# A residual addition moved from VectorE to TensorE and ScalarE, in the attention across heads of a fused two-layer kernel

## The reference

```python
x = x + attn_b(layernorm(x))
def attn_b(x):                       # 16 heads of 8 features
    q = x @ Wq + bq
    k, v = split((x @ Wdown + bdown) @ Wup + bup)
    ...  # rope turns all heads of a token alike, so it drops out of q.k and the kernel leaves it out
    att = einsum('bthd,btgd->bthg', q, k) / sqrt(8)   # per token, head against head
    att = softmax(att, axis=-1)
    out = einsum('bthg,btgd->bthd', att, v)
    return out.reshape(B, T, D) @ Wout + bout
```

## Time and profile before

| | |
|---|---|
| Time, median of 3 runs | 1090.13 us (1087.06 to 1095.89) |
| The profiled execution's own time | 1098.24 us |
| Its span | 1096.5 us |
| Mean granted TensorE clock | 0.955 of full speed |
| TensorE (PE) busy | 967.1 us, 88% |
| VectorE (DVE) busy | 768.2 us, 70% |
| GpSimd (POOL) busy | 734.9 us, 67% |
| ScalarE (ACT) busy | 697.7 us, 64% |
| The addition, L1451 | 32 times, 0.28 us each, from 645.2 to 882.4 us |

### The profile page before, as it was taken

How to read it: one execution, slowest core, us unless ns; L and a number is a source line. 1 busy time by engine, 2 the same in 40 slices (tenths; PEclk the granted TensorE clock), 3 DMA queues, 4 the chain that set the end, 5 groups by cost and what they waited for, 6 DMA issues and landing times.

```text
span 1096.5 us, 28680 instructions
## 1 busy us (share of the span) xinstructions
PE 967.1 (88%) x9400; PEld 756.2 (69%) x9402; DVE 768.2 (70%) x2246; ACT 697.7 (64%) x2121; POOL 734.9 (67%) x1070
## 2 busy tenths in 40 slices
PE   4999999999999897979999989888988749799995
PEld 2555555555556546879999567776766649799995
DVE  3678788888888964635455589899998956344454
ACT  3487877877787764535555567677676645365553
POOL 8664567777676245766666868689999666666564
PEclk8699999999999988989999999899999969899998
DMA  9999984000000005656786299999000056567883
GB/s 338 407 405 406 402 231 150 10 14 14 10 22 12 12 26 165 180 168 189 231 252 186 70 408 406 407 402 301 21 13 21 21 155 185 166 192 215 257 239 102
DMA packets 121872, 203.13 MB, mean 185 GB/s; under 512 B 13300, under 2 KB 67248, under 8 KB 121598
## 3 DMA queue, kind: packets, MB, share of 16 engines
q1 hardware_dynamic: 111470, 184.08, 50.4%
q0 software_dynamic: 9728, 16.95, 4.6%
q10 hardware_dynamic: 528, 0.26, 0.1%
HBM read 76.72 MB, written 127.65 MB: 186 GB/s over the span
## 4 chain that ended last, share of the span: by engine, by line
PE 40%; POOL 19%; DVE 17%; issue 14%; ACT 6%; DMA 1%; POOLq 1%; SPq 1%; DVEq 0%; ACTq 0%
POOL rows_out L1078 12%; PE bank L1740 6%; PE bank L1339 5%; PE bank L1701 5%; PE bank L1661 3%; DVE NMP L1923 3%; POOL SETTLE L1077 3%; POOL rows_in L718 3%; DVE QK L1445 3%; PE bank L1682 3%; PE bank L1656 2%; PE bank L1133 2%; PE bank L1144 2%; PE bank L1719 2%; ACT bank L1400 2%
## 5 line engine op out<-in xcount | busy, mean ns | idle before, releaser
L1110 ACT ACTIVATE QT<-bank,B 128x128 f32<-128x128 f32 x704 | 200.9, 368 | 170.3 <-PE bank L1133 169.4
L1865 ACT ACTIVATE PT<-bank 128x512 f32<-128x512 f32 x320 | 188.3, 603 | 75.2 <-PE bank L1682 74.8
L1078 POOL DMA_INDIRECT rows_out<-Y,XI x176 | 175.2, 995 | 73.3 <-POOL SETTLE L1077 66.1
L1133 PE MATMUL bank<-XIT,PT 128*128 128x128 f32 x1408 | 194.2, 282 | 6.8 <-DVE XIT L1214 6.5
L1144 PE MATMUL bank<-W,QT 128*128 x1408 | 190.5, 279 | 1.3 <-ACT QT L1110 1.3
L1133 PEld LDWEIGHTS bank<-XIT,PT 128*128 128x128 f32 x1408 | 175.2, 196 | 10.6 <-DVE XIT L1214 8.6
L1144 PEld LDWEIGHTS bank<-W,QT 128*128 128x128 f32 x1408 | 175.2, 196 | 1.6 <-issue 1.6
L1275 POOL TENSOR_TENSOR PT<-PT 128x512 f32<-128x512 f32 x128 | 157.9, 1266 | 27.4 <-ACT PT L1384 27.1
L718 POOL DMA_INDIRECT rows_in<-XG,POS x128 | 126.6, 989 | 41.4 <-issue 35.2
L1701 PE MATMUL bank<-KT,QT 48*128 48x384 bf16 (+3 forms) x512 | 123.5, 312 | 13.1 <-DVE NMP L1919 8.3
L1219 DVE TENSOR_TENSOR YB<-bank,B2R 128x128 f32<-128x128 f32 x176 | 51.3, 291 | 110.8 <-PE bank L1144 109.3
(11 more groups left out here) (275 smaller groups left out, 1957.0 us busy)
## 6 DMA issues: line engine op xcount, KB each, us to landing
rows_in<-XI SPq DMA_DIRECT2D x32, 3120.0 KB, 30.9
PT<-in_w_dram SPq DMA_DIRECT2D x176, 256.0 KB
XI<-rows_in SPq DMA_DIRECT2D x176, 65.0 KB
PT<-rows_out SPq DMA_DIRECT2D x31, 256.0 KB, 3.8
W<-in_w2pack_dram SPq DMA_DIRECT2D x4, 1536.0 KB
rows_in<-XI SPq DMA_DIRECT2D x2, 1560.0 KB, 31.3
rows_out<-Y,XI POOLq DMA_INDIRECT x176
X<-in_h_dram SPq DMA_DIRECT2D x8, 256.0 KB, 5.1
```

The costliest lines, as they stand in the source:

```text
L1078: pool.indirect_dma_start(out=rows_out, out_offset=bass.IndirectOffsetOnAxis(ap=XI_I[:, u, D + 1:D + 2], axis=0), in_=Y[:, u % 4, :], in_o ...
L1110: a = act.activation(HT[:, u % 2, c, :], psH[u % 2][:, c * P:(c + 1) * P], ACT.Gelu, bias=B1[:, bass.ds(e * FC + c, 1)])
L1133: mm = pe.matmul(psH[u % 2][:, c * P:(c + 1) * P], W1[:, u, c * P:(c + 1) * P], XIT[:, u % 2, :], start=True, stop=True)
L1865: act.activation(PT[:, m % PT_SLOTS, :], psB[m % 2][:, :], ACT.Exp, scale=float(D) ** -0.5).then_inc(exp_done, 1)
```

## The change

VectorE's addition is taken out. TensorE adds the tile of X, multiplied by the identity IDF, as a third product to the projection's group in PSUM, ahead of which every fourth tile waits for f_done. ScalarE copies the finished sum from psF to X, in slot T for tile T-3, ahead of the exponentials of tile T, and gives b_x. `row_at(X, T)` is tile T of X as 128 x 128.

```diff
             def project_out(T, s):
                 pe.wait_ge(b_wvt, T + 1)
                 pe.matmul(psF[:, 0:D], BWVT[:, s % 2, :], BO_W[:, :], start=True, stop=False)
-                pe.matmul(psF[:, 0:D], ONESB[0:3, :], BO_B, start=False, stop=True).then_inc(b_o, 1)
+                pe.matmul(psF[:, 0:D], ONESB[0:3, :], BO_B, start=False, stop=False)
+                if T % GT == 0:
+                    pe.wait_ge(f_done, 2 * (T // GT + 1))
+                pe.matmul(psF[:, 0:D], IDF[:, :], row_at(X, T), start=False, stop=True).then_inc(b_o, 1)
...
                 if s % GT == 2 and routed(g - 2):
                     keep_scaled(act, GROUPS + g - 2, GT * (g - 2))
+                if exists(T - 3):
+                    act.wait_ge(b_o, T - 2)
+                    act.activation(row_at(X, T - 3), psF[:, 0:D], ACT.Copy).then_inc(b_x, 1)
                 if exists(T):
                     exps(T, s)
...
         def attb_dve(dve):
-            def tile_at(x, T):
-                return x[:, bass.ds(T, 1), :].rearrange("p a d -> p (a d)")
-
...
                     dve.tensor_reduce(AMX[:, s % 2, :], ATT[:, s % 2], AX.X, ALU.max, negate=True).then_inc(b_max, 1)
-                if exists(T - 3):
-                    dve.wait_ge(b_o, T - 2)
-                    dve.tensor_tensor(tile_at(X, T - 3), tile_at(X, T - 3), psF[:, 0:D], ALU.add).then_inc(b_x, 1)
                 if exists(T - 1):
```

## The result

The changed kernel takes 1097.72 us (median of 18 runs, 1095.82 to 1099.18), the kernel before 1093.02 us (18 runs, 1085.94 to 1099.60). The ratio is 1.0039, with a 95% interval of 1.0020 to 1.0058: **slower by 0.4%, about 4 us**. A second set of runs on one chip gave 1.0033 (1.0005 to 1.0060). The forecast was +1.7 us, within 1%. Its 1091.8 us stood on the 1090.13 us of three runs; over 18 runs the kernel before has 1093.02, so it is the difference that has to be compared: measured, it is more than twice the forecast.

The account below looks back on a forecast made before the run. TensorE and ScalarE were taken to set the pace up to 719 us, GpSimd to 848 us, then VectorE. +3.26 us up to 848 us and -1.55 us after gave +1.7 us on 1090.13, so 1091.8 us, range 1084 to 1100.

Parts of the forecast that it names:

- TensorE's product: One float32 identity product per tile, 0.25 us each; +1.33 us over six early intervals up to 685.54 us.
- ScalarE's copy: One PSUM to SBUF copy per tile ahead of the exponentials, charged 0.16 us each.
- VectorE's relief: VectorE loses 32 additions, each worth 0.20 us from start to next start, and its waits for the projection.
- about 9 us less: Sign to look for in the profile after: VectorE busy about 9 us less in total and idle more.
- Four tiles in the middle: From 719 to 848 us the chain's four tiles grow 0.26 us, 31.91 to 32.17, still under GpSimd's 32.34.
- GpSimd sets the pace there: From 719 to 848 us GpSimd never waits for another engine and sets the pace, 32.34 us per four tiles.
- the other chain: Waits through TensorE, ScalarE and VectorE from projection to projection; reaches 848 us at +3.26, GpSimd at 2.6 to 2.9.
- The end, -1.55 us: From 848 us VectorE is bare: 0.60 from three additions, about 0.55 at 870.54, 0.40 among the tables.
- The sum: Whole kernel: +3.26 us up to 848 us less 1.55 us at the end, +1.7 us.
- The clock: Halving of TensorE's clock in the profiled execution; the forecast shift depends on it by at most 1 us.
- VectorE was the bound: Faster rival: VectorE limits the loop, so 12.7 us go, to 1077.4 us; chance 0.08.
- the way over TensorE and ScalarE: Slower rival: projection to exponentials bounds every tile, 0.41 us a tile, 1101 to 1103 us; chance 0.12.

Follow-up runs that it names:

- the experiment with VectorE's copy: The changed kernel, but VectorE copies the finished sum back to X instead of ScalarE; 1096.83 us, 1.0030 of the kernel before.
- no product: The changed kernel without TensorE's product with the identity, so ScalarE copies the bare projection to X; 1093.02 us, 1.0014 of the kernel before.
- copy in the wait: The changed kernel with ScalarE's copy moved from ahead of the exponentials to just ahead of the latents; 1093.76 us, 1.0016 of the kernel before.
- nobody adds: Addition, product and copy all left out, X keeps its old tokens; 1090.93 us, 0.9999 of the kernel before.
- the filling: The changed kernel plus ten products of zeros in TensorE's idle time ahead of tile 30's total; 1095.02 us, 1.0033 of the kernel before.
- the product in the gap: Copy moved ahead of the latents, and TensorE's tokens product put first, in its wait for ScalarE's transposed values; 1088.09 us, 0.9968 of the kernel before.

## Why the prediction was right

The time was inside the range and the kernel got slower, as forecast, but the measured difference is more than twice the +1.7 us, and the agreement of +1.7 with the undisturbed tiles is in part luck. Step by step:

- **TensorE's product**, 0.25 us a tile where it is on the way: measured 0.22 (6.79 to 7.01, and the experiment with VectorE's copy). The six early distances grew by 1.1 us; forecast 1.33.
- **ScalarE's copy**, 0.16 us ahead of the exponentials: measured 0.16 (no product: 7.91 to 8.07; copy in the wait: 8.29 to 8.14). The chain pays the start-to-start distance, not the duration. The Trainium skill, "VectorE: DVE Perf Modes", section on the TRN2 errata, counts 172 cycles plus one per element for ScalarE from PSUM, by estimate 0.25 us at its 1.2 GHz; the trace agrees as to the duration (0.25).
- **VectorE's relief**, 0.20 us an addition: measured 0.20 (nobody adds: 7.46 to 7.26 and 7.80 to 7.60), on two tiles of four. The "about 9 us less" busy for VectorE counted durations (32 x 0.28) that overlap; measured are 6.2, close to 32 x 0.20.
- **Four tiles in the middle**: forecast + 0.26, to 32.17; measured + 0.19, to 32.10.
- **GpSimd sets the pace there** failed as I put it. "GpSimd never waits for another engine" held in the profile I had read (the two later ones have short waits there), but it does not follow that it sets the pace: only that it is the slowest, while the others go on ahead of it as long as their buffers last. VectorE had waited for it 0.9 us in all. The forecast was saved by carrying the other chain along and taking the later of the two. That chain was put at +3.26 us at 848 us; undisturbed it was 1.1 + 5 x 0.19 = +2.1, mainly because I had let four tiles grow as if all of them ran over TensorE and ScalarE, which they did in that profile behind a halving of the clock.
- **The end, -1.55 us**, was mis-sized. Undisturbed, the last five distances shrink from 31.96 to 31.36, by 0.6, and from VectorE's sums at 847.32 us to the last row send it is 53.6 us before and 53.1 with the filling. At the addition of 870.54 I had let 0.55 us of the saved wait stay saved; but TensorE was the one waited for, and its total, one product later, holds the weighted values instead: VectorE waits 0.4 us there with the filling, 1.9 and 2.0 where the total ran at half clock.
- **The sum.** Undisturbed, the loop is 234.0 - 232.5 = 1.5 us longer; forecast +1.7. That the two agree is luck in part: the loss up to 848 us was put about 1.2 us too large and the gain behind it about 1 us too large, and the errors cancel.
- **The clock** was the term that was too small: I had allowed at most 1 us. The halvings cost 3.2 us more in the changed kernel on average, and 1.5 + 3.2 agrees in size with the measured 4 to 5 us. Three profiles each, with 2.4 to 5.4 and 4.8 to 8.3, indicate this and do not prove it. Also, the three profiled executions of the kernel before (1098.24, 1096.47 and 1093.67 us) are slow ones of their kind, and by their whole times the changed kernel's are only 0.9 us longer: the kernel before lost 3.8 us more than the changed one outside the loop. The granted clocks of whole runs point the same way, to a higher price and not to more halvings: the twelve runs of the changed kernel's repeat have a mean of 0.954, the 35 of the kernel before 0.956; with the filling it is 0.956 against 0.957, and the ratio is still 1.0033.

What stays open is how much of the measured difference the dearer halvings make up over all runs. With the product in the gap TensorE does the same work, and that profile shows only one disturbed pair of tiles between the first and the last copy (230.15 us against 229.6 undisturbed), of 0.6 us; it is an execution faster than its median, 1085.71 us.

The rival "VectorE was the bound" fell with the kernel in which nobody adds. The rule that moving work from a saturated VectorE to ScalarE may make sense (the Trainium skill, "Perfetto Trace Analysis", Optimizing Scalar/DVE Operations) held only once the moved pieces stood in the receivers' own waits. The rival "the way over TensorE and ScalarE" held in its place and price (0.38 us a tile, forecast 0.41), but on two tiles of four: in the others VectorE still has the chain.

## What to carry to other kernels

When several engines are nearly full, moving an operation is worth what it frees on the chain minus what it adds there, tile by tile; here 0.37 and 0.20 us freed against 2 x 0.38 us added in every four tiles. It also costs the room that the receiver had: what disturbs a busier TensorE is no longer hidden behind its waits, and the same halving of its clock cost twice as much. The place on the receiving engine matters more than the engine: the same product and the same copy cost 0.22 and 0.16 us ahead of the work that others wait for, and nothing inside the receivers' own waits. An engine that never waits is not yet the bound: look for who waits for it.

## What the runs showed of the hardware

Undisturbed tiles of a hand-ordered pipeline repeat to 0.01 or 0.02 us from kernel to kernel, so a difference of 0.2 us in one tile is plain in one profile, while the time of a run scatters by 10 us and more (the kernel before: 1084.58 to 1101.86 over the two sets of runs). The scatter goes with the granted clock: of the 35 runs of the kernel before beside the changed one the five fastest have 0.958 to 0.960, the five slowest 0.941 to 0.953. The clock is at half in stretches of 3.4 us, which come at other places in profiles of one and the same kernel. A single one in the middle adds 1.0 to 1.6 us in the changed kernel (8.60 + 7.18 in place of 7.09 + 7.60 us, for one) and 0.1 to 0.5 in the kernel before (8.42 + 7.33 in place of 7.46 + 7.80). Eight float32 products that took 2.05 us took 3.63 after TensorE had stood idle for 2.6 us, and 2.05 again when that idle time was filled with products of zeros.
